# Narrow attentions of a gated eight-block decoder: one set of banks for the scores, one for the turned probabilities, and the next tile's scores ahead of the last pair's weighing

## What is computed

```python
q = (layernorm(x) @ Wq + bq) split into 16 heads      # layer 2: Wq folded into the keys, no bias
s = q @ k.T * scale                                   # 16 heads x 77 keys
s = where(mask == 0, -1e20, s)                        # layer 2 alone
x = x + tanh(g) * (softmax(s) @ v @ Wo + bo)
```

## Time and profile before

| | us |
|---|---|
| median of 3 runs | 3427.18 (3418.02 to 3429.24) |
| the profiled execution, its own time | 3428.99 |
| its span, first to last instruction | 3427.7 |
| unprojected attention, first score to last statistics | 2097.0 to 2273.2 |
| projected attention, first score to last statistics | 2550.5 to 2711.0 |

### The profile page before, as it was taken

One profiled execution on the slowest core, in us unless ns is written; L12 is line 12 of the kernel. 1 busy time (PEld: TensorE's weight loads), 2 busy tenths in 40 slices (PEclk: granted clock), 3 DMA queues, 4 the chain that ended last, 5 costly groups with the idle time before them and its releaser, 6 DMA issues.

```text
span 3427.7 us, 38700 instructions
## 1 busy us (share of the span) xinstructions
PE 3141.8 (92%) x14674; PEld 2176.6 (64%) x14674; DVE 1853.4 (54%) x3026; ACT 1190.0 (35%) x2206; POOL 629.9 (18%) x958
## 2 busy tenths in 40 slices
PE   7989899999999999999999998779978699995996
PEld 5668677677667767776666665655647544553564
DVE  5986788568666855773211015643236556665213
ACT  4333323542463255222222212321224345552332
POOL 1206301000100010011100002320434321111453
PEclk9999999999999999999999998879989979997998
DMA  5100100010010001000100000002730011011633
GB/s 133 59 1 1 52 1 1 13 64 1 1 52 25 1 13 42 23 1 1 49 13 25 1 0 19 1 13 106 245 120 1 20 32 44 29 42 73 223 115 110
DMA packets 85390, 150.95 MB, mean 44 GB/s; under 512 B 26357, under 2 KB 62743, under 8 KB 80471
## 3 DMA queue, kind: packets, MB, share of 16 engines
q1 hardware_dynamic: 70327, 77.15, 7.3%
q0 software_dynamic: 14880, 71.33, 6.0%
HBM read 173.14 MB, written 17.56 MB: 56 GB/s over the span
## 4 chain that ended last, share of the span: by engine, by line
PE 77%; DVE 11%; DMA 3%; ACT 3%; issue 3%; POOL 2%; SPq 0%; ACTq 0%; POOLq 0%; DVEq 0%
PE psum L391 10%; PE psum L414 9%; PE psum L1576 6%; PE psum L1564 6%; PE psum L1238 6%; PE psum L1250 6%; PE psum L2055 4%; PE psum L2076 2%; DVE row L2885 2%; PE psum L685 2%; PE psum L381 2%; PE psum L936 2%; PE psum L427 2%; DMA L_results<-shared,prep 2%; PE psum L2209 2%
## 5 line engine op out<-in xcount | busy, mean ns | idle before, releaser
L391 PE MATMUL psum<-Vt,shared 128*128 128x256 f32 (+1 forms) x1600 | 368.1, 385 | 12.8 <-ACT shared L552 11.9
L391 PEld LDWEIGHTS psum<-Vt,shared 128*128 128x128 f32 (+1 forms) x1600 | 300.4, 192 | 69.2 <-issue 31.0
L414 PE MATMUL psum<-Kt,xnTt 128*128 128x512 f32 (+1 forms) x960 | 343.9, 508 | 0.5 <-ACT xnTt L497 0.5
L414 PEld LDWEIGHTS psum<-Kt,xnTt 128*128 128x128 f32 x960 | 179.4, 189 | 158.6 <-issue 153.4
L2885 DVE TENSOR_REDUCE row<-psum 128x1 f32<-128x128 f32 (+7 forms) x256 | 188.0, 754 | 124.3 <-PE psum L2634 122.1
L1250 PEld LDWEIGHTS psum<-expert_w,prep 128*128 128x128 f32 x1024 | 194.6, 190 | 78.1 <-issue 57.9
L1250 PE MATMUL psum<-expert_w,prep 128*128 128x256 f32 x1024 | 240.8, 379 | 0.0
L1238 PE MATMUL psum<-weights,expert_w 128*128 128x512 f32 x512 | 240.3, 593 | 0.0
L381 PE MATMUL psum<-ident,shared 128*128 128x128 f32 x1120 | 155.0, 289 | 76.1 <-POOL shared L808 62.3
L2774 ACT ACTIVATE prep<-psum 128x512 f32<-128x512 f32 (+3 forms) x384 | 171.3, 490 | 148.3 <-PE psum L2656 147.7
L1138 DVE SCALAR_TENSOR_TENSOR bias<-Kt,small,bias 128x1232 f32<-128x1232 f32 x96 | 149.2, 1554 | 129.7 <-ACT Kt L1122 128.4
(11 more groups left out here) (399 smaller groups left out, 6028.0 us busy)
## 6 DMA issues: line engine op xcount, KB each, us to landing
expert_w<-in_L_xattn_Wf SPq DMA_DIRECT2D x16, 512.0 KB, 5.7
weights<-q_parts SPq DMA_DIRECT2D x32, 144.0 KB
weights<-k_parts SPq DMA_DIRECT2D x96, 48.0 KB
weights<-in_L_xattn_Wk SPq DMA_DIRECT2D x4, 1024.0 KB, 5.0
weights<-in_L_xattn_Wv SPq DMA_DIRECT2D x4, 1024.0 KB, 7.1
weights<-in_L_xattn_Wq SPq DMA_DIRECT2D x4, 1024.0 KB, 5.4
weights<-in_L_xattn_Wo SPq DMA_DIRECT2D x4, 1024.0 KB, 5.3
weights<-in_L_ffn_w SPq DMA_DIRECT2D x8, 512.0 KB, 4.8
```

Source lines behind the costliest of these rows:

```text
L391: ins = pe.matmul(o_bank(t), probT[0:rows, t % 2, c, :], Vt[0:rows, t // TB, c, :], start=(c == 0), stop=(c == CH - 1))
L414: ins = pe.matmul(flat[:, par * 3 * BANK + at:par * 3 * BANK + at + cols], xnTt[:, par, k, :], Kt[:, t // TB, k, src:src + cols], start=(k ...
```

## The change

Scores now always go to banks 0 to 2 and turned probabilities to banks 3 to 5, whatever the tile's number. PE's wait for `p_kept` ahead of the scores becomes a wait for `shifted` of the tile before, and the turning of probabilities gets waits of its own on `p_kept`, group by group. PE weighs the pair before behind the scores of t + 1 and the turning of tile t + 2, no longer ahead of them. ACT keeps tile t + 2 ahead of the weighed pair. No instruction is added or removed. The wide attentions, which run before, keep the old function for turning.

```diff
+    NARROW_TURNED = 3 * BANK
...
         def scores(t):
...
-            if t >= 2:
-                pe.wait_ge(p_kept, 3 * (g0 + t - 1))
+            if t >= 1:
+                pe.wait_ge(shifted, g0 + t)
             for bank in NARROW:
                 for at, cols, parts in bank:
                     for k, src in parts:
-                        ins = pe.matmul(flat[:, par * 3 * BANK + at:par * 3 * BANK + at + cols],
-                                        lhs[:, par, k, :], Kt[:, t // TB, k, src:src + cols],
+                        ins = pe.matmul(flat[:, at:at + cols], lhs[:, par, k, :], Kt[:, t // TB, k, src:src + cols],
                                         start=(k == parts[0][0]), stop=(k == parts[-1][0]))
             ins.then_inc(scored, 1)
+
+        def turn_probabilities(t):
+            pe.wait_ge(weights_made, g0 + t + 1)
+            for b0 in range(0, CH, 4):
+                if t >= 1:
+                    pe.wait_ge(p_kept, 3 * (g0 + t - 1) + b0 // 4 + 1)
+                for c in range(b0, min(b0 + 4, CH)):
+                    rows = min(P, HK - c * P)
+                    ins = pe.transpose(flat[0:rows, NARROW_TURNED + c * P:NARROW_TURNED + (c + 1) * P],
+                                       prob[:, t % 2, c * P:c * P + rows], ident[:, :])
+                ins.then_inc(p_turned, 1)
...
         for t in range(NT):
-            if t % 2 == 0 and t >= 2:
-                weigh(t // 2 - 1)
             if t + 1 < NT:
                 scores(t + 1)
             if t + 2 < NT:
                 turn_tile(t + 2)
-            pe_turn_probabilities(pe, n, t)
+            if t % 2 == 0 and t >= 2:
+                weigh(t // 2 - 1)
+            turn_probabilities(t)
...
         for t in range(NT):
-            par, base = t % 2, t % 2 * 3 * BANK
+            par, base = t % 2, NARROW_TURNED
             act.wait_ge(shifted, g0 + t + 1)
             act.activation(prob[:, par, :], prob[:, par, :], ACT.Exp, scale=scale).then_inc(powered, 1)
+            if t + 2 < NT:
+                keep_tile(t + 2)
             if t % 2 == 0 and t >= 2:
                 keep_outputs(t // 2 - 1)
-            if t + 2 < NT:
-                keep_tile(t + 2)
...
-            src = flat[:, par * 3 * BANK:par * 3 * BANK + HK].rearrange("p (h c) -> p h c", h=H)
+            src = flat[:, 0:HK].rearrange("p (h c) -> p h c", h=H)
```

## The result

| | changed kernel | kernel before |
|---|---|---|
| median, first comparison (13 runs each) | 3433.63 us (3423.54 to 3441.71) | 3422.67 us (3415.80 to 3432.84) |
| ratio to the kernel before | 1.0030, 95% interval 1.0018 to 1.0043 | |
| same instructions again (12 and 17 runs) | 3428.92 us | 3425.74 us |
| ratio | 1.0009, 95% interval 0.9998 to 1.0021 | |
| profiled execution, its own time | 3429.81 us | 3428.99 us |

The change makes the kernel at most a few microseconds slower: the first comparison puts it 0.3% above the kernel before, with an interval that excludes no change, and the second cannot tell it from no change. The attentions do not differ so: their times are the same in both traces of the changed kernel, to 0.1 us.

What follows compares the result with a forecast made beforehand. It took chains of waits through DVE, ACT, POOL and PE, plus low clock, to bound the attentions. From 3428.99, -0.6 (unprojected) and +3.6 (projected) gave 3432.0, less 1.8 to the median: 3430.2 us, range 3418 to 3440.

Steps and rivals of the forecast that it cites:

- The full-clock round of 18.2 us: Unprojected attention: length of one round, a pair of tiles, in the new order if the clock stays up.
- The low clock: Unprojected attention: half-speed PE clock would likely persist, landing on odd scores and part of weighing, adding 2.2 us a round.
- These edges: Start, last pair and moved steps outside the repeating rounds: together put at 0 us.
- 0.2 more than the old round at full clock: Unprojected attention: the new round at full clock takes 18.2 us, the old one 18.0.
- ACT's queue: Unprojected attention: the odd exponential waits behind ACT's in-order copies of even probabilities, bringing weighing back onto its path.
- Over six rounds that is 4.3 us if the extras stay as they are: Projected attention: 0.72 us more a round, 18.16 against 17.44; +3.6 us taken, from 0.9 to 4.3.
- the extras: Projected attention: 3.5 us over six clean rounds, in rounds with extra DVE or POOL work or a low clock.
- A: Rival: low clock becomes regular in the projected attention, 10 to 20 us lost over six rounds, 3440 to 3450; chance 0.12.
- B: Rival: unprojected attention keeps full clock, rounds of 18.2 us, -14.0 us over six, kernel 3416.8 us; chance 0.08.
- C: Rival: earlier scores pay because ACT's late exponential costs nothing; DVE bounds a pair, kernel 3403 to 3415 us; chance 0.02.

Runs made afterwards that it cites:

- fill: Changed kernel plus 26 unread identity turnings a pair in PE's pauses of the unprojected attention; ratio 0.9977 to the kernel before, that attention 160.1 us.
- fill_before: Kernel before plus 32 unread identity turnings a pair in PE's one pause of the unprojected attention; ratio 0.9965 to the kernel before, that attention 166.5 us.
- early: Changed kernel, but unprojected scores wait for the previous tile's mask addition, not its subtraction; ratio 0.9940 to the kernel before, that attention 150.1 us.
- mix: Changed kernel with unprojected scores waiting only for the mask addition and projected odd exponentials before ACT's copies; ratio 0.9878 to the kernel before, 3383.34 us.
- order_only: Changed kernel's order on the old two sets of banks; ratio 0.9987 to the kernel before, attentions 165.8 us (unprojected) and 167.4 us (projected).
- ahead: Changed kernel with ACT's odd exponential before its copies of weighed pair and even probabilities, both attentions; ratio 0.9920 to the kernel before, attentions 160.6 and 151.3 us.

## Why the prediction was right, and where it was off

**The unprojected attention: the mechanism held, the total with some luck.** Forecast 20.4 against 20.53 a round, -0.6 us (six times the difference would be -0.8); measured 176.1 against 176.2, -0.1 us. The full-clock round of 18.2 us is 18.18 in fill. The low clock costs 20.57 - 18.18 = 2.4 us a round where I took 2.2, and lies on the scores (4.53 us) as argued. Counted by the subtractions of odd tiles, the last six rounds take 123.4 us against 123.2, so they did not get shorter; what lies ahead of them takes 2.6 us less and what lies behind them 2.3 us more. These edges I had put at 0, and they nearly cancel. The old round at full clock, put at 18.0, is 18.4 in fill_before, so "0.2 more than the old round at full clock" has the wrong sign. What the working missed is what else would have freed the round. It named ACT's queue as the one thing in the way, and early took 26 us out without touching ACT's order: the scores' wait for the subtraction stands in the same chain, and I had counted it as given.

**The projected attention: right mechanism, term too small.** Forecast +3.6 us, measured +5.9 (166.4 against 160.5), and the same in the second trace. The round was forecast at 18.16 and the clean ones are 18.18. "Over six rounds that is 4.3 us if the extras stay as they are" was put as the upper end, and that step failed: two extras grew, against clean rounds of 17.4 before and 18.2 now. The round with the low clock went from 19.0 to 21.2, because the low stretch there lasts 6.8 us instead of 3.4 and now covers scores that are waited for (4.49 us in the chain). DVE's four extra tiles of rows fell behind the start of the second weighing before, in a round of 18.3; now they fall ahead of it, in the first round, and make it 19.3. I had them better covered, but the turning of tile t + 2 waits for DVE behind them and the weighing now stands behind that turning. In the chain it is this piece (267 normalises, 366 turns):

```profile
2594.70 0.38 DVE meanvar L223 x4
2595.08 0.31 DVE xn L267
2595.39 0.04 issue
2595.44 0.44 PE psum L366 x2
2595.88 4.75 PE psum L698 x22
```

The third and the first round give 2.2 + 1.9 us. The four others sum to 72.6 us against 71.7, 1.0 more: two of the old ones were at 18.3 already, one through DVE's extra rows, one through POOL's extra work, which the longer round absorbed. That makes 5.0 of the 5.9 us; the last weighing, 6.06 us in the low clock against 5.23, gives most of the rest.

**The sum.** 3.0 us slower than the median shown was forecast. The stage times say 5.9; the first comparison says 10 (6 to 15), the second 3 (-1 to 7). The stretch behind the attentions varied from 705 (mix) to 721 us (order_only) between the traces of kernels that are alike there. I take the first comparison's surplus as scatter of that kind. It isn't shown: no trace was at hand of an execution as slow as 3440 us.

**The rivals.** A (low clock in every projected round) did not come: one such stretch in the middle rounds, as before, only longer. B (full clock in the unprojected attention) did not come by itself; fill forces it and gives 18.2 us a round, B's price. Of the two statements weighed from "TensorE: Matmul & The Clock Gate" in the Trainium skill, the one in "A second HAM failure mode: psum-queue depth-cycling" agrees with the trace: pauses of 2.02 and 2.35 us with a burst between them went with a clock that fell in each round, and with work in both pauses (fill) it stayed at 1.00. The one in "Why this matters for your kernels", long pauses alone, does not describe the changed kernel, whose longest pause in the round shown is 2.35 us. C (ACT's order costs nothing) is refuted by the late exponential in the trace and by ahead.

## What to carry to other kernels

When work moves off one path in a hand-ordered program, follow every engine's queue behind it: here the weighing left the odd scores' path and came back through ACT's in-order copies, and one exponential moved ahead of them was worth 15 us in the projected attention, with the new order as it is. Release a buffer at its last reader, not at the next counter that happens to exist: 2.9 us earlier gave 26 us, some 12 of them by itself and the rest with the low stretches that it shortened. Where PE pauses in each round, cost a new order at full clock and at the observed clock apart; a gain may only move the low stretch onto work that is waited for.

## What was not expected of the hardware

With a low stretch in each round the rounds of both kernels settle at the same length, though their chains differ: 20.63, 20.56, 20.51 and down to 20.49 us before, 21.21, 20.85, 20.67 and down to 20.53 in the changed kernel, from subtraction to subtraction. Whether the clock sets that length is not shown; at full clock they take 18.4 and 18.2. Idle work for PE paid for itself: with 26 extra turnings of the identity a pair in its pauses, fill's clock stays at 1.00 over 127 us, and the attention takes 160.1 us against 176.1. Two traces of the changed kernel agree to 0.1 us in such a stage, while its whole time varies by 18 us between runs (3423.54 to 3441.71).
